# A new prologue for a four-layer kernel: where the first head group gets its rows, and in which order

## What is computed

```
ql, ckv = xn @ Wqd, xn @ Wkvd                     # latents, 64 wide
q, k, v = ql @ Wqu, ckv @ Wku, ckv @ Wvu          # "nope" parts, 16 per head
qr = rope(ql @ Wqr)   # 64 per head               # rotated queries
kr = rope(xn @ Wkr)   # 64, one for all heads     # rotated key
scores = (q.k + qr.kr) * scale; softmax over s <= t; out = attn @ v @ Wo
```

## Time and profile before

| what | us |
|---|---|
| median of 3 runs (lowest, highest) | 992.88 (991.86, 996.1) |
| profiled execution, its own time | 994.7 |
| its span in the trace | 993.0 |
| TensorE busy | 862.0 (87%) |
| VectorE, ScalarE, GpSimd busy | 555.9, 386.8, 224.9 |
| first maxima product of group 0 | at 48.95 |
| first score product of group 0 | at 87.71 |
| first score products of groups 1, 2, 3 | at 157.77, 194.84, 245.17 |

### The profile page before, as it was taken

The page is one execution under the profiler, slowest core; times in us unless marked ns, Lnnn a source line. Parts: engine busy times, 40 slices in busy tenths (PEclk is TensorE's granted clock), DMA queues, the critical chain, the costliest instruction groups (busy, mean ns, idle before and its releaser), DMA issues.

```text
span 993.0 us, 11940 instructions
## 1 busy us (share of the span) xinstructions
PE 862.0 (87%) x4799; PEld 505.4 (51%) x4799; DVE 555.9 (56%) x991; ACT 386.8 (39%) x476; POOL 224.9 (23%) x207
## 2 busy tenths in 40 slices
PE   4697979988999899987779998788999889888997
PEld 2354434444344434524448886533333258687776
DVE  4574486774677476512433453596777337934452
ACT  2504314534444454445351331205555754500340
POOL 2661002323013212523010100500111147600000
PEclk9878999999799889979789997968999989989899
DMA  6687216514721770020400002759000061000001
GB/s 174 130 174 225 34 33 107 112 49 105 129 34 43 145 179 2 2 71 1 149 0 1 1 1 88 147 108 130 2 2 1 2 222 43 0 1 1 1 1 43
DMA packets 35648, 66.82 MB, mean 67 GB/s; under 512 B 5908, under 2 KB 14652, under 8 KB 35524
## 3 DMA queue, kind: packets, MB, share of 16 engines
q1 hardware_dynamic: 35016, 65.92, 29.0%
q10 hardware_dynamic: 576, 0.13, 0.1%
HBM read 45.93 MB, written 16.29 MB: 63 GB/s over the span
## 4 chain that ended last, share of the span: by engine, by line
PE 63%; DVE 19%; DMA 6%; ACT 6%; POOL 2%; issue 2%; SPq 1%; ACTq 0%; DVEq 0%; POOLq 0%
PE psA L1604 11%; PE psD L1604 11%; PE psO L1725 10%; DVE mx L1204 9%; PE psD L1670 8%; PE psA L1688 7%; PE psO L1604 7%; PE psA L1687 3%; DMA Kr<-d_kn 3%; DVE hid_low L1518 2%; PE psD L1672 2%; PE psA L1636 1%; SPq L488 1%; ACT Pr L912 1%; PE psD L1736 1%
## 5 line engine op out<-in xcount | busy, mean ns | idle before, releaser
L1204 DVE TENSOR_REDUCE mx<-psD 128x1 f32<-128x512 f32 (+3 forms) x416 | 259.3, 659 | 122.9 <-PE psD L1672 88.3
L912 ACT ACTIVATE Pr<-psA 128x1024 f32<-128x1024 f32 (+3 forms) x192 | 161.9, 865 | 194.9 <-PE psA L1688 185.4
L781 POOL TENSOR_SCALAR_AFFINE_SELECT Pr<-Pr 128x512 f32<-128x512 f32 x96 | 61.0, 635 | 435.6 <-ACT Pr L912 349.6
L917 ACT ACTIVATE Pr<-psA 128x1024 f32<-128x1024 f32 (+3 forms) x96 | 63.5, 702 | 65.4 <-PE psA L1688 65.0
L1725 PE MATMUL psO<-Pr,Vh 128*32 128x512 f32 (+3 forms) x768 | 81.9, 507 | 3.7 <-POOL Pr L781 3.0
L1687 PE MATMUL psA<-Qr,Kr 128*128 128x512 f32 (+3 forms) x192 | 77.5, 417 | 3.7 <-DMA Qr<-mrow 3.7
L1672 PE MATMUL psD<-maskq,identb 128*128 128x128 bf16 x348 | 73.0, 234 | 0.0
L1688 PE MATMUL psA<-Qr,Kr 113*128 113x512 f32 (+3 forms) x192 | 66.5, 354 | 0.0
L1670 PE MATMUL psD<-Kg,Qs 96*128 96x512 bf16 (+3 forms) x192 | 56.2, 333 | 9.0 <-DVE mx L1204 6.9
L1670 PE MATMUL psD<-Kr,Qr 80*128 80x512 bf16 (+3 forms) x166 | 59.2, 390 | 5.2 <-DVE mx L1204 3.0
L1688 PE MATMUL psA<-Qs,Kg 97*128 97x512 bf16 (+3 forms) x192 | 51.3, 366 | 9.5 <-DMA Qs<-mrowb 4.3
(11 more groups left out here) (403 smaller groups left out, 1658.6 us busy)
## 6 DMA issues: line engine op xcount, KB each, us to landing
Qr<-d_qr SPq DMA_DIRECT2D x18, 512.0 KB, 12.3
d_qr<-WB SPq DMA_DIRECT2D x9, 512.0 KB, 2.6
Pr<-d_cb SPq DMA_DIRECT2D x8, 512.0 KB, 7.8
Qs<-d_gq SPq DMA_DIRECT2D x24, 128.0 KB, 4.8
Qs<-d_q SPq DMA_DIRECT2D x24, 128.0 KB
Ks<-d_k SPq DMA_DIRECT2D x24, 128.0 KB
Qr<-d_qn SPq DMA_DIRECT2D x18, 128.0 KB, 7.7
Kr<-d_kn SPq DMA_DIRECT2D x18, 128.0 KB, 8.5
```

The lines of the kernel that those rows point to most:

```text
L781: pool.affine_select(out=block_, in_=block_, pattern=[[0, GH], [1, P]], compare_op=ALU.is_ge, fill=0.0, base=0, channel_multiplier=-1).the ...
L912: act.activation(place[:, h, q0:T], src[:, q0:T], ACT.Exp, scale=score_scale(i)).then_inc(a_drained, 1)
L917: act.activation(place[:, h:h + 2, q0:T], src[:, :, q0 - HALF:HALF], ACT.Exp, scale=score_scale(i)).then_inc(a_drained, 1)
L1204: dve.tensor_reduce(mx[:, j, part, h0:h0 + nh], src, AX, ALU.max).then_inc(d_drained, 1)
```

## The change

- **Loads of x** have a semaphore per pair of row tiles, and the statistics of a pair wait for that pair.
- **TensorE runs on zeros**: GpSimd clears `otmp` first, and TensorE runs 36 products of 128x512 bf16 on it before it waits for the identity matrix.
- **Order and engines**: the key product comes before the latents. GpSimd makes `wq_low` (it was VectorE). ScalarE cuts the rotated key straight into Kr for heads 0 and 1, cuts both nope tiles as soon as they are there and copies them in full later. VectorE adds rope 0 itself. Qr2's high rows are one copy of ScalarE in place of a DMA.
- **Nope rows** of head group 0 go from SBUF to SBUF, one DMA per head and row block; the stores to DRAM (needed for the later groups) come behind. Kr's heads 2 and 3 and Kr2 are copied from Kr's heads 0 and 1.
- **First maxima**: `first_max_units` yields the 20 units of heads 0 and 1, then the 20 of heads 2 and 3. The first half waits for rope pair 0 and `first_in[0]`, the second for pair 1, `first_in[1]` and `kr_in`.
- **Ropes** 2 to 7 lie at (group, kt) = (0,0), (0,1), (1,5), (2,0), (3,5), (4,0). Pair 3's second buffer is a slot of Qs instead of Pr; VectorE waits before pair 3 for all nope stores. GpSimd's and ScalarE's steps and the stores of pairs 2 and 3 move into group 0.
- **Key and maxima**: `KEY_KT` is 2, and `max_end` is 4 for groups 3, 5 and 7.
- **Selected key/value**: TensorE writes the features in the order (s, d, h), reading `w_qkv0` with a step of 16 floats, so that VectorE's sum over h is contiguous.

```diff
 def max_end(g):
-    return 5
+    return 4 if is_shared(g) and g > 1 else 5

-ROPE_AT = {(2, 0): 4, (2, 2): 5, (4, 0): 6, (4, 2): 7}
+ROPE_AT = {(0, 0): 2, (0, 1): 3, (1, 5): 4, (2, 0): 5, (3, 5): 6, (4, 0): 7}
 KV_AT = {(0, 0): range(0, NT // 2), (0, 1): range(NT // 2, NT)}
-KEY_KT = 3
+KEY_KT = 2
...
-        PRE0 = [("lat",), ("kr",), ("nope", 0), ("nope", 2)] + [("rope", p) for p in range(4)]
+        PRE0 = [("kr",), ("lat",), ("nope", 0), ("nope", 2), ("rope", 0), ("rope", 1)]
...
+            def place_nope(u, part, heads, row, s):
+                t = (Qr, Kr)[u // 2]
+                for h in heads:
+                    load(slot(t, h, HD, row).bitcast(F32), nope_place(u)[part][h * HD:(h + 1) * HD, :], s)
+            sp.wait_ge(nope_cut, 1)
+            place_nope(0, 0, (0, 1), RD, first_in[0])
+            sp.wait_ge(nope_cut, 2)
+            place_nope(2, 0, (0, 1), RD, first_in[0])
+            sp.wait_ge(kr_ready, 1)
+            load(Kr[0:RD, 2 * T:4 * T]..., Kr[0:RD, 0:2 * T]..., kr_in)
+            for u in (0, 2):
+                place_nope(u, 0, (2, 3), RD, first_in[1])
+            load(Kr2[RD:2 * RD, :].bitcast(F32), slot(Kr, 0, RD).bitcast(F32), kr2_in)
...
+                elif p == 3:
+                    dve.wait_ge(nope_stored, 16 * 8)
...
+                if p == 0:
+                    dve.wait_ge(d_drained, n[0])
+                    v, b = rope_place(p)
+                    dve.tensor_tensor(v, v, b, ALU.add).then_inc(first_sum, 1)
...
+            act.wait_ge(kr_sum, 1)
+            act.activation(slot(Kr, 0, RD), kr, ACT.Copy)
+            act.activation(slot(Kr, 1, RD), kr, ACT.Copy).then_inc(kr_ready, 1)
+            srcs = [take(), take()]
+            for n_, u in enumerate((0, 2)):
+                act.activation(nope_place(u)[0].bitcast(F32R), srcs[n_], ACT.Copy).then_inc(nope_cut, 1)
+            act.activation(nope_place(0)[1], srcs[0], ACT.Copy).then_inc(a_drained, 1)
+            rope_cut(0)
+            act.activation(nope_place(2)[1], srcs[1], ACT.Copy).then_inc(a_drained, 1)
+            rope_cut(1)
...
+                by_dim = lambda k: w_qkv0[:, k, D:3 * D].rearrange("p (s h d) -> p s d h", s=2, h=H)
+                product(d_unit().rearrange("p (s d h) -> p s d h", s=2, h=H),
+                        [(xnT[:, k, tile_cols(j)], by_dim(k)) for k in range(DC)]).then_inc(d_filled, 1)
...
+                zeros = otmp[:].rearrange("p j h d -> p (j h d)").bitcast(BF16)
+                for _ in range(count):
+                    pe.matmul(psO[:, 0:HALF], zeros[:, 0:P], zeros, start=True, stop=True)
+            pe.wait_ge(spare_ready, 1)
+            keep_running(36)
```

More of the change, by code:

```diff
@@ L52, with first_max_units @@
 MAX_UNITS = list(max_units())
+def first_max_units():
+    for h0 in (0, 2):
+        for j in range(NT):
+            for part in range(1 + (j >= NT // 2)):
+                w = min(HALF, (j + 1) * P) if part == 0 else (j + 1) * P - HALF
+                nh = 2 if w <= 2 * P else 1
+                for h in range(h0, h0 + 2, nh):
+                    yield j, part, h, nh, w
+FIRST_MAX = list(first_max_units())
 def max_end(g):
-    return 5
+    return 4 if is_shared(g) and g > 1 else 5
 def is_mla(i):
@@ L72, in head_group @@
     return i // 2 if i < 2 * NG else i - 2 * NG
-ROPE_AT = {(2, 0): 4, (2, 2): 5, (4, 0): 6, (4, 2): 7}
+ROPE_AT = {(0, 0): 2, (0, 1): 3, (1, 5): 4, (2, 0): 5, (3, 5): 6, (4, 0): 7}
 KV_AT = {(0, 0): range(0, NT // 2), (0, 1): range(NT // 2, NT)}
-KEY_KT = 3
+KEY_KT = 2
 def beside_products(i, kt):
-    if (i, kt) in KV_AT:
-        return [("kv", j) for j in KV_AT[i, kt]]
+    products = [("kv", j) for j in KV_AT.get((i, kt), ())]
     if (i, kt) in ROPE_AT:
-        return [("rope", ROPE_AT[i, kt], k) for k in range(4)]
+        products += [("rope", ROPE_AT[i, kt], k) for k in range(4)]
     if (i, kt) == (2 * NG - 1, 1):
-        return [("wdn", u) for u in range(FC // 2)]
-    return []
+        products += [("wdn", u) for u in range(FC // 2)]
+    return products
 def max_window(i, first):
@@ L493, in _ @@
             for j in range(0, NT, 2):
[L494 removed]
+                load(x[:, j:j + 2, :], ins["x"].rearrange("(j p) d -> p j d", p=P)[:, j:j + 2, :], x_in[j // 2])
             load(identf[:], ins["c_ident"], ident_in)
@@ L559, in _ @@
[L559 to L568, removed]
@@ L580, in store_rotated @@
                 rope_store(p, 1)
-            store_rotated(2)
-            store_rotated(3)
+            for u in (0, 2):
+                for part in range(2):
+                    nope_store(u, part)
+            sp.wait_ge(split_done, 1)
+            load(d_gq[:, tile_cols(0), :].rearrange("s d t -> d s t"), split_place(0)[1], split_stored[0])
             for u in (1, 3):
@@ L746, in nope_rest @@
                 pool.tensor_tensor(v.bitcast(F32R), v, high_part, ALU.subtract).then_inc(nope_low, 1)
-            for p in range(4):
-                rope_add(p)
             nope_rest(0)
+            rope_add(1)
             nope_rest(2)
-            for p in range(4):
-                rope_rest(p)
+            rope_rest(0)
+            rope_rest(1)
             def split_step(u, k, done=split_done):
```

109 lines of the change are left out of this document (59 added, 50 removed).

## The result

The changed kernel takes 976.84 us (median of 4 runs, 976.72 to 977.93), the kernel before 993.2 beside it: ratio 0.9834, 95% interval 0.9811 to 0.9857. It is faster, inside the range that I gave, but by 16.4 us and not by 35. The profiled execution took 976.76 us, its span is 975.0.

What follows compares the result with a forecast made beforehand. TensorE bounds the kernel (63% of the path), with gains where it idles or runs at lower clock. Terms -14.7 + 3.8 - 5.3 + 0 - 3.0 - 18.0 + 2.0 = -35.2 from 994.7, less 1.8: 958 us, range 946 to 979.

Steps and rivals of the forecast that it cites:

- Prologue, -14.7: Everything before group 0's first score: group 0 starts at 73.0 instead of 87.7 us; bounds -20 and -9.
- VectorE's add is held by GpSimd until 34.0: Prologue, adding rope 0's halves: collides with GpSimd's nope subtraction and ends at 34.0, not 32.7, 1.3 us later.
- my 36.8: Prologue, first score to group 0's start: 36.8 us against 38.8 before, shared-query features cold again, value products partly faster.
- Ropes 2 and 3, +3.8: Group 0's key tiles 0 and 1: these ropes move in from the prologue where TensorE is busy, costing 3.8 us.
- key and maxima, -5.3: Group 0's key tiles 2 to 4: shared key earlier, group 1's maxima over three tiles, 32.0 us instead of 37.3.
- Selected products, 0: Group 0's selected key/value products: weights read with a step of 16 floats cost nothing; bounds 0 and +13.8 us.
- The rival with 0.24: Group 0's selected products: strided weight reads slow the passes, up to twice as long, +13.8 us; chance 0.24.
- the boundary rival: Boundaries of groups 2 to 3 and 4 to 5: TensorE still runs dry, clock falls, +18, 976 us; chance 0.14.
- Ropes -3.0: Groups 2 and 4: moving ropes 4 to 7 out of tile 2 removes stalls beside the outputs, -3.0 us (0 to -5).
- boundaries -18.0: Starts of groups 3 and 5: earlier loads and maxima end remove the row wait and low clock, -18.0 us (0 to -20).
- denser maxima +2.0: Groups before 3, 5 and 7: their maxima, ending a tile earlier, are 12% denser, costing 2.0 us (0 to +6).
- the first two rivals: Strided reads in group 0's selected products (up to +13.8 us, chance 0.24) and stalls remaining at group boundaries (+18, chance 0.14).

Runs made afterwards that it cites:

- e8: The changed kernel with the shared key in group 0's key tile 3 again and group 1's maxima in key tiles 3 and 4 alone: 981.8 us, ratio 0.987.
- e2: The kernel before with only the selected products' part changed (weights read with a step of 16 floats, VectorE's sum contiguous): 1003.2 us, ratio 1.010.
- e5: The changed kernel with the maxima of groups 3, 5 and 7 running to key tile 4 again: 972.9 us, ratio 0.978.
- e13: The kernel before with only the places of the four later pairs of ropes changed: 974.5 us, ratio 0.982.
- e3_write: The changed kernel with the selected products' weights read contiguously and PSUM written with the step of 16 floats: 964.4 us, ratio 0.971.

## Why the prediction was right in sign and wrong in size

- **Prologue, -14.7: right in size, in part by luck**, -14.1: the first score was 1.5 us early and the stretch behind it 2.1 late. Steps: products at 15.34 (16.1 forecast), nope products done at 28.2 (28.4), first score 34.71 (36.2), group 0 at 73.62 (73.0).
- The step **"VectorE's add is held by GpSimd until 34.0" fell**, and the 1.3 us that I had put on it: the add ended at 32.5. They start within 0.01 us of each other, VectorE first, and GpSimd is the one stretched:

```profile
31.23 1.22 DVE L1223 TENSOR_TENSOR Pr<-Pr 128x1024 f32<-128x1024 f32 x1
31.24 3.43 POOL L771 TENSOR_TENSOR Qs<-Qs 128x1024 fp32r<-128x1024 f32 x1 [2.48 <-ACT Qs L1006]
...
20.52 2.25 DVE L1379 TENSOR_TENSOR xn<-xn 64x1024 f32<-64x1024 f32 x1
17.17 4.52 POOL L753 TENSOR_TENSOR wq_low<-WA,wq_high 128x2048 fp32r<-128x2048 f32 x1 [2.95 <-ACT wq_high L996]
```

  The key's add at 20.52, behind a GpSimd subtraction that had started at 17.17, is held to 22.8. Who starts first goes through. I had GpSimd start 0.8 us earlier, ahead of the add. The section of the Trainium skill that the prediction names (SBUF — State Buffer, "SBUF: two separate sides") says this too (the first to start gets the pair for its whole instruction); I used half of it.
- From the first score to group 0 took 38.9, 2.1 over my 36.8: the shared-query features were cold as said, but took 5.80 us and not 5.3, and TensorE was cold again from 47.7 to 57.9, as long as in the kernel before (64.9 to 75.2). The value products, 16 passes, did get back the half that I had counted (4.54 us against 6.06), but maxima units ahead of them ran cold in their place.
- **Ropes 2 and 3, +3.8; key and maxima, -5.3**: about right. e8 gives 4.4 for the second. For the first, e8 and e2 differ in group 0 by these ropes above all: 85.2 - 82.5 = 2.7; no run moved them alone.
- **Selected products, 0: wrong, and the largest miss**, 11.1 to 12.4 us. I took the end of the bounds that the nearest row of the same instruction gave, but that row had the contiguous read, the one thing that changed. The argument "half rate, so there may be room" was sound only for a factor of two (a step of 2 floats is free); the step was 16. The rival with 0.24 was the right one, near the full price that it left open. The time itself, 976.8, is the one that the boundary rival gave (976), but its mechanism did not occur: the clock stayed at 1.00 behind the starts of groups 3 and 5.
- **Ropes -3.0, boundaries -18.0, denser maxima +2.0**, together -19.0: measured -14.2. The reason that I gave for the 2.28 us, "the maxima end a tile earlier", fell in e5; the loads that can leave early, my other half of the same step, carry it all (e13: 264.4 to 246.9, -17.5, for my -21.0). The early end has only its cost, 3.6 for my 2.0.
- Sum of the misses: about 11.5 (products) + 3.5 (ropes and boundaries) + 1.6 (denser maxima) + 0.6 (start) = 17. By stretch it is 0.6 (start) + 12.3 (group 0) + 4.8 (groups 1 to 6) - 0.4 (the rest) = 17.3. The forecast change in the trace was -35.2, the measured one 976.76 - 994.7 = -17.9.
- The ends of my range do not follow from what I named for them: the low bounds of prologue and group 0 give 958 - 5.3 - 1.7 = 951 and not 946, and the first two rivals give 970 and 976 one by one, some 990 together, and not 979.

## What to carry to other kernels

Price a changed access pattern by the operand that changes, not by the nearest row of the same instruction; if no row has it, the pattern's own arithmetic (on how many new 16 bytes its elements fall) is a better guide than the old duration, and one short run settles it. When a trace names a small DMA as what an engine waited for, look at what was issued just ahead of it: here the fault lay in loads chained to a rope two tiles before. And let one edit at a time prove itself: the change's best part (the ropes' places, 17.5 us alone in e13) came with two that cost 12 and 3.6.

## What the runs showed of the hardware that I had not expected

- TensorE's read of its moving operand (the one that is streamed): about 1.7 ns for each new 16 bytes, and a pass takes the longer of this and its streaming; fp32 512 columns 0.43 us at steps of 1 and 2, 0.86 from 4 to 32; bf16 runs 0.22 contiguous, 0.45 at a step of 4 and 0.9 at a step of 8 elements. A strided unit took 3.62 us at clock 0.50 and 3.59 at 1.00.
- A PSUM write with a step of 64 bytes cost nothing: 645 ns a pass in e3_write, as in the kernel before.
- VectorE and GpSimd, both reading two SBUF operands: the later one waits, 2.25 us instead of 1.22 for VectorE, 3.43 instead of 2.4 for GpSimd.
